# A Swin block and a depthwise convolution on one core: the second MLP layer computed transposed, onto the turned residual, with the engines' orders and PSUM banks dealt anew

## The reference

```
xn   = layer_norm(x, ln1)                      # over 96 channels
wins = windows(roll(xn, -3, -3))               # 7 x 7 tokens each
q, k, v = wins @ qkv_w + qkv_b
attn = softmax(q k^T / sqrt(32) + rel_bias + mask)
x    = x + roll_back((attn v) @ proj_w + proj_b)
y    = gelu(layer_norm(x, ln2) @ fc1_w + fc1_b)    # 96 -> 384
x    = x + y @ fc2_w + fc2_b                       # 384 -> 96
x    = depthwise3x3(relu(x), dw_kernel) + dw_bias
x    = batch_norm(x @ pw_kernel + pw_bias)
```

## Time and profile before

| | |
|---|---|
| median of 3 runs | 6512.59 us (6494.89 to 6518.01) |
| profiled execution | 6505.5 us |
| its span, first to last instruction | 6503.7 us |
| TensorE (PE) busy | 5885.1 us, 90% |
| VectorE (DVE) busy | 5637.3 us, 87% |
| ScalarE (ACT) busy | 5164.0 us, 79% |
| GpSimd (POOL) busy | 3072.3 us, 47% |
| mean granted TensorE clock | 0.987 of full |
| DMA | 10% busy, 26 GB/s |

### The profile page before, as it was taken

One profiled execution on the slowest core, in us unless ns is written; L12 is line 12 of the kernel. 1 busy time (PEld: TensorE's weight loads), 2 busy tenths in 40 slices (PEclk: granted clock), 3 DMA queues, 4 the chain that ended last, 5 costly groups with the idle time before them and its releaser, 6 DMA issues.

```text
span 6503.7 us, 219980 instructions
## 1 busy us (share of the span) xinstructions
PE 5885.1 (90%) x88850; PEld 4606.4 (71%) x88850; DVE 5637.3 (87%) x14257; ACT 5164.0 (79%) x11040; POOL 3072.3 (47%) x4105
## 2 busy tenths in 40 slices
PE   6999999999999999999999999999999999999997
PEld 4777777777777777777777777777777777777775
DVE  4888888888888888888888888888888888888887
ACT  4888788888878888888888887878888888888785
POOL 3444444444444444444444444444444444445452
PEclk8999999999999999999999999999999999999998
DMA  0111111111111111111111111111111111110100
GB/s 21 26 26 26 26 26 26 26 26 26 26 26 26 26 26 26 26 26 26 26 26 26 26 26 26 26 26 26 26 26 26 26 26 26 26 27 25 28 25 19
DMA packets 250594, 169.04 MB, mean 26 GB/s; under 512 B 220423, under 2 KB 220920, under 8 KB 249592
## 3 DMA queue, kind: packets, MB, share of 16 engines
q1 hardware_dynamic: 249592, 154.97, 9.3%
HBM read 77.81 MB, written 77.07 MB: 24 GB/s over the span
## 4 chain that ended last, share of the span: by engine, by line
PE 66%; DVE 14%; POOL 12%; ACT 4%; issue 3%; SPq 1%; DVEq 0%; DMA 0%; POOLq 0%; ACTq 0%
PE bank L376 17%; PE bank L392 15%; PE bank L422 8%; POOL rstd L881 6%; DVE stats L773 5%; PE bank L452 5%; PE bank L407 5%; POOL x1n L887 5%; PE bank L478 4%; DVE x L819 4%; PE bank L359 4%; PE bank L464 3%; PE bank L344 3%; PE bank L440 3%; ACT attnT L596 2%
## 5 line engine op out<-in xcount | busy, mean ns | idle before, releaser
L757 DVE SCALAR_TENSOR_TENSOR acc<-ymap,taps,acc 96x784 f32<-96x784 f32 (+2 forms) x2176 | 2428.3, 1121 | 45.7
L881 POOL TENSOR_TENSOR rstd<-var_eps,minus_half 112x7 f32<-112x7 f32 x512 | 919.5, 1796 | 3267.0 <-DVE var_eps L788 3267.0
L376 PE MATMUL bank<-x1T,w 96*128 96x448 f32 (+1 forms) x3072 | 1178.0, 523 | 1.5 <-ACT x1T L561 1.2
L392 PE MATMUL bank<-w,hT 128*112 128x96 f32 x10752 | 1099.1, 262 | 0.0
L392 PEld LDWEIGHTS bank<-w,hT 128*112 128x112 f32 x10752 | 1077.9, 178 | 0.6
L376 PEld LDWEIGHTS bank<-x1T,w 96*128 96x128 f32 x3072 | 559.9, 195 | 516.9 <-issue 336.8
L573 ACT ACTIVATE hT<-bank,bfc 128x448 f32<-128x448 f32 (+1 forms) x1536 | 829.3, 576 | 47.6 <-PE bank L376 35.3
L866 POOL TENSOR_TENSOR prob<-prob,smax 128x392 f32<-128x392 f32 x768 | 804.6, 1079 | 21.9 <-DVE smax L726 21.9
L551 ACT ACTIVATE x1n<-x,offset,rstd 112x96 f32<-112x96 f32 x1024 | 394.8, 456 | 388.8 <-POOL offset L884 388.8
L819 DVE TENSOR_TENSOR x<-bank,x_in 112x384 f32<-112x384 f32 (+1 forms) x512 | 250.1, 507 | 468.4 <-PE bank L478 468.4
L875 POOL TENSOR_TENSOR prob<-prob,srec 128x392 f32<-128x392 f32 x768 | 633.2, 855 | 38.6 <-DVE srec L735 38.6
(11 more groups left out here) (89 smaller groups left out, 10996.5 us busy)
## 6 DMA issues: line engine op xcount, KB each, us to landing
out<-o_tile SPq DMA_DIRECT2D x256, 210.0 KB, 2.5
x_in<-in_x SPq DMA_DIRECT2D x256, 168.0 KB, 2.9
x_in<-in_x SPq DMA_DIRECT2D x256, 126.0 KB, 3.3
out<-o_tile SPq DMA_DIRECT2D x256, 84.0 KB, 2.5
hT<-in_L_conv_rel_bias SPq DMA_DIRECT2D x49, 0.6 KB
x1T<-in_L_conv_fc_w SPq DMA_DIRECT2D x1, 144.0 KB, 2.4
w<-in_L_conv_fc_w SPq DMA_DIRECT2D x1, 144.0 KB, 2.3
hT<-in_L_conv_qkv_w SPq DMA_DIRECT2D x1, 108.0 KB, 2.1
```

The lines of the kernel that those rows point to most:

```text
L376: pe.matmul(bank[5 + i % 3][:, 0:n * PT_], w1[:, m * 128:(m + 1) * 128], x1T[:, first * PT_:(first + n) * PT_], start=True, stop=True).the ...
L392: mm = pe.matmul(bank[half][0:PT_, a * C:(a + 1) * C], hT[:, m, j * PT_:(j + 1) * PT_], w2[:, m, :], start=(m == 0), stop=(m == MC - 1))
L757: last = dve.scalar_tensor_tensor(out=dst, in0=src, scalar=taps[:, i:i + 1], in1=dst, op0=ALU.mult, op1=ALU.add)
L881: pool.tensor_tensor(b["rstd"][:], b["var_eps"][:], minus_half[0:PT_], ALU.pow)\
```

## The change

**MLP.** `second_layer` is split in two calls, one for each half. Each first turns the residual `x1` into the bank (4 or 3 transposes, as `turn_y` did), then adds the second layer on top: w2 is stationary, the hidden activations stream, 3 matmuls of 448 or 336 columns for each half, accumulated. The result already has channels on partitions. `add_x1` on VectorE and `turn_y` on TensorE are gone, with their semaphores; `into_map` reads the second layer's banks.

**Orders.** TensorE: both halves of the values come before the turning of x1n; the pointwise product is split, the first half before `hidden`, the second after the turning of xn; the turning of xn comes in one piece after the weighing of the values. ScalarE: both key copies before the normalisation; `outputs` is split, the first half before the gelus, the second after the attention output; `into_map` is split around the probability copies; both halves of xT come last. VectorE: tap 4 moves behind the row sums. GpSimd: `root` is split in `root` (power and offset) and `rest` (three columns); the `rest` of the first normalisation moves behind the divisions.

**Banks and areas.** The banks are dealt anew, with the waits that go with them; five banks are cleared at the start instead of three. The map has six areas, three of which take turns, and `into_map` of strip t - 1 waits for the last tap of strip t - 4.

```diff
-AREAS = 5
+AREAS = 6
...
             def scores(t):
-                wait(pe, xt_ready, nth(t + 1, 2, 1))
-                wait(pe, y_ready, nth(t - 2, 2, 1))
                 wait(pe, pt_ready, nth(t - 1, 3, 0))
+                wait(pe, ymap_ready, nth(t - 2, 2, 0))
+                wait(pe, out_ready, nth(t - 5, 2, 1))
...
-            def second_layer(t):
-                for half, (first, n) in enumerate(((0, 4), (4, 3))):
-                    wait(pe, h_ready, nth(t - 1, 6, 3 * half + 2))
-                    for a in range(n):
-                        j = first + a
-                        for m in range(MC):
-                            mm = pe.matmul(bank[half][0:PT_, a * C:(a + 1) * C], hT[:, m, j * PT_:(j + 1) * PT_],
-                                           w2[:, m, :], start=(m == 0), stop=(m == MC - 1))
-                    mm.then_inc(y_psum, 1)
+            def second_layer(t, half):
+                first, n = ((0, 4), (4, 3))[half]
+                b = (1, 7)[half]
+                if half == 0:
+                    wait(pe, x1t_ready, nth(t - 1, 2, 1))
+                    wait(pe, x1_ready, nth(t - 1, 2, 1))
+                else:
+                    wait(pe, v_ready, nth(t + 1, 2, 0))
+                    wait(pe, ymap_ready, nth(t - 2, 2, 1))
+                for a in range(n):
+                    pe.matmul(bank[b][0:C, a * PT_:(a + 1) * PT_], x1[:, first + a, :], ident[0:PT_, 0:PT_],
+                              is_transpose=True, start=(a == 0), stop=False)
+                for m in range(MC):
+                    wait(pe, h_ready, nth(t - 1, 6, 3 * half + m))
+                    mm = pe.matmul(bank[b][0:C, 0:n * PT_], w2[:, m, :], hT[:, m, first * PT_:(first + n) * PT_],
+                                   start=False, stop=(m == MC - 1))
+                mm.then_inc(y_psum, 1)
...
             def turn_probs(t, h):
                 wait(pe, p_ready, nth(t, 3, h))
...
+            def turn_x(t):
                 wait(pe, xn_ready, nth(t + 2, 1, 0))
                 wait(pe, xn_rest, nth(t + 2, 1, 0))
+                for i, (js, perm, b) in enumerate(((range(3, 7), ident[0:PT_, 0:PT_], 3), (range(0, 3), roll[:], 4))):
+                    wait(pe, pt_ready, nth(t, 3, i + 1))
+                    wait(pe, q_ready, nth(t + 1, 2, i))
+                    wait(pe, v_ready, nth(t + 1, 2, 1))
+                    wait(pe, out_ready, nth(t - 4, 2, 0))
+                    for a, j in enumerate(js):
+                        mm = pe.transpose(bank[b][0:C, a * PT_:(a + 1) * PT_], xn[:, j, :], perm)
+                    mm.then_inc(xt_psum, 1)
...
@@ TensorE @@
             def step(t, phase):
                 scores(t)
                 queries_keys(t)
                 values(t, 0)
+                values(t, 1)
                 turn_x1(t)
-                values(t, 1)
+                pointwise(t, phase, 0)
                 hidden(t, 0)
                 hidden(t, 1)
-                pointwise(t, phase)
-                second_layer(t)
-                turn_x(t, 0)
+                second_layer(t, 0)
+                second_layer(t, 1)
                 if has(t):
                     for h in range(HEADS):
                         turn_probs(t, h)
-                turn_x(t, 1)
-                if has(t):
                     for h in range(HEADS):
                         weigh_values(t, phase, h)
-                turn_y(t)
+                turn_x(t)
+                pointwise(t, phase, 1)
                 project(t)
...
@@ ScalarE @@
             def step(t, phase):
                 queries(t)
+                keys(t, 0)
+                keys(t, 1)
                 if has(t - 1):
                     wait(act, x1t_psum, nth(t - 2, 2, 1))
                     normalise(1, t - 1, x1n, x1, x1n_ready)
-                keys(t, 0)
                 x1_turned(t)
-                keys(t, 1)
+                outputs(t, phase, 0)
                 gelus(t)
                 for g in range(3):
                     exps(t, g)
                 if has(t + 2):
                     wait(act, xt_psum, nth(t + 1, 2, 1))
                     normalise(0, t + 2, xn, x_in[:, (phase + 2) % UNROLL], xn_ready)
-                outputs(t, phase)
-                x_turned(t, 0)
+                into_map(t, 0)
                 for h in range(HEADS):
                     probs_turned(t, h)
+                into_map(t, 1)
+                attention_out(t)
+                outputs(t, phase, 1)
+                x_turned(t, 0)
                 x_turned(t, 1)
-                attention_out(t)
-                into_map(t, phase)
...
@@ VectorE, step @@
                 tap(t, phase, 3)
-                tap(t, phase, 4)
                 for g in range(3):
                     add_up(t, g)
-                add_x1(t)
-                for i in range(5, 9):
+                for i in range(4, 9):
                     tap(t, phase, i)
                 add_x(t, phase)
...
@@ GpSimd @@
             def step(t, phase):
                 if has(t - 1):
+                    root(1, t - 1)
                     wait(pool, x1t_psum, nth(t - 2, 2, 1))
-                    root(1, t - 1, x1n, x1, x1n_rest)
-                shift(t, 0)
-                shift(t, 1)
-                shift(t, 2)
+                    rest(1, x1n, x1, x1n_rest)
+                for g in range(3):
+                    shift(t, g)
+                if has(t + 2):
+                    root(0, t + 2)
+                for g in range(3):
+                    divide(t, g)
                 if has(t + 2):
                     wait(pool, xt_psum, nth(t + 1, 2, 1))
-                    root(0, t + 2, xn, x_in[:, (phase + 2) % UNROLL], xn_rest)
-                for g in range(3):
-                    divide(t, g)
+                    rest(0, xn, x_in[:, (phase + 2) % UNROLL], xn_rest)
```

More of the change, by code:

```diff
@@ L444, in pointwise @@
+            def pointwise(t, phase, i):
                 if not has(t - 4):
                     return
[L446 to L449 removed]
+                first, n = HALVES[i]
+                if not has(t):
                     wait(pe, out_ready, nth(t - 5, 2, i))
[L451 to L454 removed]
@@ L468, in project @@
+                for a in range(n):
+                    mm = pe.matmul(bank[(4, 2)[i]][0:HW, a * C:(a + 1) * C], acc[:, phase % 2, first + a, :], wpw[:],
+                                   start=True, stop=True)
+                mm.then_inc(pw_psum, 1)
             def project(t):
@@ L614, in into_map @@
                 s = t - 1
-                wait(act, tap_done, nth(t - 3, 9, 8))
+                first, n = ((0, 4), (4, 3))[half]
+                if half == 0:
+                    wait(act, tap_done, nth(t - 4, 9, 8))
                 area = area_of_strip(s)
@@ L885, in root, with rest @@
                     .then_inc(scale_ready[which], 1)
+            def rest(which, dst, src, done):
+                b = ln[which]
                 for j in range(ACT_NORM, WS):
```

150 lines of the change are left out of this document (55 added, 95 removed).

## The result

The changed kernel takes 6517.24 us, the median of 20 runs (6512.83 to 6530.41), against 6506.27 of the kernel before beside it (6494.72 to 6518.01, 20 runs). The ratio is 1.0019, with 1.0012 to 1.0026 as its 95% interval: 11 us slower, less than the 0.5% that the prediction took as the bound of "same". It had said 6560, and it gave this outcome a chance of 0.18.

The account below looks back on a forecast made before the run. Bound: a loop over 256 strips in which engines wait for each other. 9.19 + 15.88 = 25.07 against 24.77, +76 us over 255 steps; 6505.5 + 76 - 20 + 1 = 6562, say 6560; own range 6490 to 6640, wider 6300 to 6700.

Parts of the forecast that it names:

- the mechanism: After the row sums, VectorE's two-input taps and GpSimd's divisions and scalings shut each other out; TensorE waits for GpSimd.
- the steady step: One strip of the loop between two table loads for the gelus: forecast 25.07 us against 24.77, +0.30.
- The sample of three scalings and the subtractions: Evidence from the kernel before: three scalings beside taps took 3.49 us against 1.23 at the run's end; subtractions likewise mid-run.
- rival (a): GpSimd's scalings slip in without waiting for taps, or earlier; step 24.4 us, time 6410 us; chance 0.13.
- Rival (b): No collisions between taps and GpSimd count at all; step 23.6 to 23.8 us, time 6240 us; chance 0.10.
- (d): Each of five handings over between VectorE and GpSimd costs 0.2 us more; step 26.1 us, time 6840 us; chance 0.03.
- I take off 20, a guess between none and all: Allowance of 20 us from the 51 us the mean step had over the steady one, last strips included.
- H: Start of the first MLP layer on TensorE, forecast 9.19 us after the projection's start, as before.
- Rival (c): TensorE's clock halves in new waits around probabilities and weighing; such a step loses 1.2 us; 6620 or 6710 us; chance 0.12.
- P': Start of the next projection on TensorE, forecast at H + 15.88 us, queued behind the turning of x.
- my bound of 4.1: Lower bound in us for the second layer's 12 instructions on TensorE, forecast 4.25, upper bound 4.6.
- the turning: TensorE's turning of x after GpSimd's last scaling, forecast to start at H + 14.50 us.

Follow-up runs that it names:

- the one-input run: The changed kernel with the accumulation of taps 4 to 8 left out, so each has one SBUF input instead of two: 6289.32 us, ratio 0.9672.
- the second layer alone: The kernel before with only the MLP part of the change and its bank shifts, all orders as before: 7110.53 us, ratio 1.0936.

## Why the prediction was right and wrong

**Right: the mechanism and the steady step.** 25.07 was forecast, 25.05 came, and what should show it stood there: scalings of 3.37 us for three beside the taps (3.0 or more), the third division 1.58 (near 1.5), waits of 0.89 and 0.81 (about 0.9), 0.46 for x1n (below 0.5), and none for the attention output. The sample of three scalings and the subtractions carried; rival (a) doubted the sample and fell. Rival (b) is near what the one-input run shows, and (d), 26.1 a step, is excluded by 25.05.

**Wrong: the step "I take off 20, a guess between none and all".** It priced all that the mean step has over the steady one, 51 us before. Measured, it became -1.6: 53 off. The forecast of fewer half-clock stretches was right in kind (none of 20 left) and stood 14 us too small. The other 20 us I had not looked at: the last strip of each image, 25.45 before against a steady 24.77, went below the steady step, to 24.50. There the taps are cut in two. Before, that held the row sums up to H + 7.86, against 7.00 in the steady step; with tap 4 behind the sums they start at H + 7.30, hardly later than in the steady one. The kernel with tap 4 back in front prices this at 0.65 of the swing of 1.23 us. Behind the sums, the cut taps are ten instructions for five, and GpSimd gets in sooner:

```profile
900.81 2.85 POOL L873 TENSOR_SCALAR xn<-x_in,minus_mean,rstd 112x96 f32<-112x96 f32 x3
```

2.85 against 3.37, and the third division is shorter too (2.96 for the three against 3.19). The end behind the last mark, at nothing in the sum, gave 8.1 more: before, the last relu waited 8.36 us for taps that stand behind the adds to x1 in VectorE's order, and began 16.2 us behind the last mark; without the adds it begins 7.2 behind it. Its row before (the last mark stands at 6458.24):

```profile
6474.44 2.14 ACT L627 ACTIVATE ymap<-bank,cols 96x256 f32<-96x256 f32 x6 [8.36 <-DVE acc L757]
```

In the second layer alone, which has no adds either but keeps the five areas, the end is 40.6 against 45.5 before, so the adds are a part of it at least. With both sized right the same sum gives 6505.5 + 76 - 53 + 1 - 8 = 6521. That would have been "same". So the step that failed is this allowance of 20 us for everything beside the steady step, with nothing for the end: the runs showed 61. What was missed lay not in the collisions but in the terms next to them.

**Rival (c)** took the clock to fall in the new waits. In the changed kernel it fell in none of them. But as a danger it was real: it is what happens in the second layer alone, in nearly every step, where the way from P' to H is 2.06 us longer although the wait of 1.18 for x1n is gone from it. And it did come in the last strips of other kernels, with tap 4 in front for one. There the waits around the turnings of the probabilities are 0.28, 0.16 and 0.65 us; in the last strips of the changed kernel only the 0.65 stands. What kept the changed kernel free of it isn't settled: 11 of the 15 last strips with tap 4 in front have the same waits and no stretch. Waits of 0.89 and 0.81 with 2.6 us of work between them had none, 1.62 and 0.57 with 1.6 us between had it always, 1.11 to 1.18 before the turnings had it in one step of 13 to 15.

**Terms that were off and cancelled.** Second layer and turnings of the residual took 4.63 and not 5.13, 0.68 us for the 7 turnings from start to start and 3.95 for the 12 instructions (6 matmuls of float32), below my bound of 4.1. The reason given for a saving of next to nothing, that the same number of columns streams either way, was wrong: 21 matmuls of 96 columns are 2016, 3 x 784 are 2352, and the new form is the shorter one all the same. The first layer, with a wait of 0.38 for the gelus in it, took 4.67 and not 4.38. The sums came at H + 7.29 (7.08), the turning at 14.82 (14.50), P' at 16.08 (15.88), and from P' to H it took 8.96 (9.19): the turning of x1 comes 7.33 behind P' and not 7.47, and takes 0.85 and not 0.94. Errors of 0.2 to 0.5 left 0.02; that the sum was so much better than its terms is luck. (The prediction has the first division at H + 7.93, where its own terms, 7.08 and 0.80, give 7.88.)

## What to carry to other kernels

When the steady step is predicted well and the total is not, the loss is in what repeats seldom: take the mean interval apart into steady, clock-touched, and boundary steps before pricing it, rather than guess a share of the whole. Where GpSimd's work that others wait for runs beside an engine's row of two-input operations, and that engine has time to spare, let it wait for GpSimd: here a wait of 1.25 us on VectorE bought 0.54 us a step, and one of 2.45, with ScalarE's order changed as well, 1.62. Price a turning or a copy that looks superfluous by what it covers; taken from behind the weighing without putting other work in its place, with the banks shifted to match, it cost 9%.

## What the runs showed of the hardware

- A tap issued during the first of three back-to-back divisions waited past the two others and took 2.52 us; another time (the changed kernel) a tap and a division took turns, one by one. A strict alternation does not describe it. The Trainium skill (SBUF — State Buffer, Who interferes with whom) says that the one that starts first keeps the ports and the other is blocked; who comes next when both have more to issue it does not say, and these runs show both outcomes.
- The residual can be turned into a bank and matmuls accumulated on top of it. The 12 instructions (6 matmuls, 2352 columns streamed) of the second layer take 3.95 us where the 42 of before (21 matmuls, 2016 columns) took 4.13 from their start to that of the next group, and each turning in front of them about 0.1.
- Half-clock stretches came in lengths of 3.4 us, 6.8 and up to 20.5. In the second layer alone 6.8 us of them came in 250 of the 255 steps; in the changed kernel, with 2.54 us of waits a step in its four rows against 2.19 there, none. So it isn't the sum of the waits that decides, and where they stand matters.
- In four kernels (scalings in front, tap 4 in front, and the two with ScalarE reordered) 2 to 7 stretches began near the weighing of the values. Of these 19, 18 lie in steps of a last strip, which are 15 of the 255. In the seven with the scalings in front TensorE waited 0.68 to 0.74 us before the turnings and twice more between them, in the others 0.28 to 0.96. Other last strips with the same waits had none, so the waits alone do not tell them apart.
- In the one-input kernel four stretches, of 10.2 to 17.1 us, began within some 2 us of the end of the weighing, none in a last strip. In these four steps TensorE stood still for 1.24 to 1.70 us at the end of the weighing, and the profile names no releaser.
- Two pieces of a tap in place of one let a neighbour's three scalings through in 2.85 us and not in 3.37, with the same work done.
